# A two-layer decoder on one core: value products with the values as weights in the first attention, scores on four quarters of the array in the second cross attention, and new orders on every engine

## The chip, the core and the metric

The kernel runs on one core of a Trainium2 chip. The core has five engines that run their own instruction streams in order and meet at semaphores: TensorE (PE; its weight loads are shown apart as PEld), VectorE (DVE), ScalarE (ACT), GpSimd (POOL) and SyncE (SP), whose queue issues nearly all transfers here. The metric is device time in microseconds (us), the median of several executions. Lower is better.

## The reference

Input x is 16 batches of 64 tokens of 128 numbers. Two layers, each of three blocks, each with a layer norm ahead and a residual addition behind:

```
x = x + L0_attn(ln(x))          # causal self attention
x = x + L0_xattn(ln(x), ctx)    # one head of 128, no mask
x = x + L0_ffn(ln(x))           # 8 experts + a shared one, top 2 per token
x = x + L1_attn(ln(x))          # state space scan, gelu, layer norm
x = x + L1_xattn(ln(x), ctx)    # 8 heads of 64, key mask, projection
x = x + L1_ffn(ln(x))           # 8 experts; each takes its best tokens
```

Two of them matter here. In the first attention the 64 x 384 projections of a batch are reshaped to 16 heads, so that a head is 64 positions of 24 numbers (8 each for query, key, value):

```
qkv = (ln(x) @ W + b).reshape(b, 16, s, 24)        # q, k, v of 8 each
attn = softmax(q @ k.T * scale + causal)
out = (attn @ v).reshape(b, s, 128)
```

The second cross attention:

```
q, k, v = x @ W_q, ctx @ W_k, ctx @ W_v           # 8 heads of 64
sim = where(mask, q @ k.T * scale, -max)
out = (softmax(sim) @ v) @ W_o + b_o
```

## The kernel before

X holds all 1024 tokens on the chip as 8 tiles of 128 tokens (a tile is two batches), and half h is tiles 4h to 4h + 3. PSUM is used as eight banks of 128 x 512 floats, named bank[0] to bank[7]. Every engine's program is a list of calls of small functions, written out by hand; the order of that list is the order of the instructions, and a `wait_ge` in a function holds everything behind it on that engine. There is no scheduler.

**First attention.** It runs over eight pairs m of batches. The unit of softmax is u = 2m + u2, eight of the 16 heads of pair m: a 128 x 512 block whose partitions are two batches of 64 and whose columns are eight heads of 64. PE computes scores (L758) onto a causal bias (L749), one call for both units of a pair. DVE takes the row maximum (row_max, L1843) and subtracts it (subtract_max, L1850). ACT takes the exponentials (L1413). PE transposes them in four 128 x 128 blocks (transpose_probs, L776), always into bank 4, so that transpose_probs(u) waits until ACT has copied u - 1 out (copy_probs, L1419). Then weigh_values(u) (L792) multiplies: the probabilities of two batches by 64 positions are the weights (128 rows by 64 columns), and the moving side is Vb, the values of a head with a column of ones behind them (VW = 9 columns for each of two batches, block diagonal), 18 columns. Its output has query positions on partitions. The ones give the softmax's sum; DVE takes its reciprocal (inverse, L1829) and multiplies (normalise, L1835) into att.

Position and head then have to change places to give tokens. This goes through DRAM, once for each half: outputs_by_feature(h) transposes on PE (L804), ACT copies (L1427), SP stores to o_scratch (L418) in pieces of 128 bytes and loads back to OT (L421); outputs_by_token(h) transposes on PE (L822), and add_attention(h) on DVE adds to X (L1856). Between the two round trips SP issues the weights of the last FFN (1 MB of W1, L425, and eight pieces of W2, L427).

**Second cross attention.** It runs over the tiles t. scores1(t) starts a bank with one matmul that spreads the mask over 128 rows (L971: maskrow, on one partition, 512 columns) and adds 16 products of 64 x 64 (L976), two batches by eight heads. Head 2hp + h2 has its query and key on partition half h2 and its output on the same half h2, so of the four 64 x 64 quarters of the array only the two on the diagonal are used. DVE subtracts the row maximum (subtract_max1, L1954 and L1957) and, behind ACT's exponentials (L1488), adds up and inverts (probs1, L1964 and L1965); POOL multiplies (weigh_probs, L529); PE transposes into bank 2 (L986), ACT copies, PE multiplies by the values (weigh_values1, L999), ACT copies, PE projects (project_out, L1014) into bank 5 or 7, and DVE adds to X (add1, L1970). The DVE step that makes maskrow from the mask's bytes (mask_row, L1790) stands in DVE's list behind add_attention(1).

**Last FFN.** The choice of tokens is a search for a threshold for each expert: count (L1068) on PE and a chain of small DVE steps alternate 16 times. PE's list puts three or four up1 (L1029) or sixteen down1 (L1041) products between two counts. Behind the search DVE adds 56 weighted parts (L2042).

## Time and profile before

| what | value |
|---|---|
| three executions | 256.94, 257.46 (median), 261.43 us |
| the profiled execution: span | 255.3 us, 5508 instructions |
| median less the profiled span | 2.16 us |
| PE busy | 239.0 us (94%) |
| DVE busy | 175.9 us (69%) |
| ACT busy | 141.8 us (56%) |
| POOL busy | 77.9 us (31%) |

The profile is of one execution. Busy time is that of an engine's own instructions; a share over the span mixes stages with different limits, so the rows below are taken from stages. A group of rows in a timeline puts together instructions of one line that follow each other closely, with their count. Most fp32 matmuls of the program appear as two records (two passes), so a count in the trace is twice that of the program there; transposes appear once.

### The profile page before, as it was taken

What the parts mean: (1) busy time and instruction counts of PE and PEld (TensorE: products, weight loads), DVE (VectorE), ACT (ScalarE), POOL (GpSimd) and SP (SyncE); (2) the same over time, 40 slices, a digit from 0 to 9 for tenths busy, and PEclk for the clock granted to TensorE, in tenths of its full rate; (3) what the DMA queues carried; (4) which work ended last, traced back from release to release, by engine and by line L of the source; (5) the groups of instructions that cost most, each with busy time, mean ns of one, the idle gap of its engine ahead of it and who ended that gap; (6) DMA issues with size and microseconds to landing.
All of it is one profiled execution on the core that took longest, in us unless ns stands there. A gap on an engine that the chain in (4) does not pass through costs nothing.

```text
span 255.3 us, 5508 instructions
## 1 busy us (share of the span) xinstructions
PE 239.0 (94%) x1993; PEld 163.9 (64%) x1994; DVE 175.9 (69%) x602; ACT 141.8 (56%) x293; POOL 77.9 (31%) x137
## 2 busy tenths in 40 slices
PE   8988899998999999999999886999998999999995
PEld 8555577774535766756593534678887566577775
DVE  5465699874878836445217979957655688889975
ACT  0764776764264688467657445465565744544540
POOL 7856900001040474667465051533401000000000
DMA  5888960178100000000000000000000000000002
GB/s 136 173 196 245 302 152 0 31 220 205 44 1 0 1 3 0 0 1 3 0 1 3 1 0 0 3 3 3 3 5 0 3 0 0 1 3 0 0 3 82
DMA packets 24040, 11.64 MB, mean 46 GB/s; under 512 B 13017, under 2 KB 23006, under 8 KB 24014
## 3 DMA queue, kind: packets, MB, share of 16 engines
q1 hardware_dynamic: 22973, 10.94, 16.5%
q0 software_dynamic: 80, 0.20, 0.7%
q8 instruction: 16, 0.26, 0.4%
q10 hardware_dynamic: 960, 0.16, 0.3%
q14 instruction: 11, 0.08, 0.1%
HBM read 8.68 MB, written 2.62 MB: 44 GB/s over the span
## 4 chain that ended last, share of the span: by engine, by line
PE 73%; DVE 15%; ACT 5%; issue 3%; POOL 2%; DMA 1%; DVEq 0%; POOLq 0%; ACTq 0%
PE bank L1029 10%; PE bank L1041 10%; PE bank L897 6%; PE bank L884 6%; PE bank L916 6%; PE bank L776 3%; DVE stats L1720 3%; PE bank L1014 3%; PE bank L758 2%; PE bank L976 2%; PE bank L648 2%; PE bank L792 2%; PE bank L693 2%; PE bank L986 2%; PE bank L999 2%
## 5 line engine op out<-in xcount | busy, mean ns | idle before, releaser
L516 POOL TENSOR_TENSOR X<-X,att 128x128 f32<-128x128 f32 x72 | 30.4, 457 | 29.2 <-ACT att L1469 29.1
L441 POOL TENSOR_TENSOR rs<-rs,halves 128x4 f32<-128x4 f32 x14 | 14.9, 1063 | 61.8 <-DVE rs L1735 61.1
L1029 PE MATMUL bank<-XT,Wb 128*128 128x512 f32 x64 | 29.9, 599 | 0.0
L1041 PE MATMUL bank<-Wb,att 128*128 128x128 f32 x224 | 27.2, 278 | 0.0
L1041 PEld LDWEIGHTS bank<-Wb,att 128*128 128x128 f32 x224 | 26.1, 192 | 1.4 <-issue 1.4
L1905 DVE SCALAR_TENSOR_TENSOR att<-bank,cols,att 128x512 f32<-128x512 f32 x18 | 13.5, 749 | 16.8 <-ACT att L1458 7.8
L1469 ACT ACTIVATE att<-bank,comb 128x128 f32<-128x128 f32 x72 | 20.2, 383 | 6.9 <-PE bank L916 6.8
L1509 ACT ACTIVATE att<-bank 128x512 f32<-128x512 f32 x32 | 18.7, 599 | 9.7 <-PE bank L1029 9.7
L916 PEld LDWEIGHTS bank<-W2a,att 128*128 128x128 f32 x144 | 18.0, 192 | 5.0 <-issue 3.6
L916 PE MATMUL bank<-W2a,att 128*128 128x128 f32 x144 | 18.7, 276 | 0.0
L884 PE MATMUL bank<-XT,W1a 128*128 128x512 f32 x36 | 18.2, 595 | 0.0
L897 PE MATMUL bank<-XT,W3a 128*128 128x512 f32 x36 | 18.1, 598 | 0.0
L1517 ACT ACTIVATE big<-bank 128x512 f32<-128x512 f32 x14 | 8.3, 596 | 17.1 <-PE bank L1041 17.1
L1458 ACT ACTIVATE att<-bank,cols 128x512 f32<-128x512 f32 x18 | 12.6, 699 | 9.5 <-DVE att L1905 7.1
L1029 PEld LDWEIGHTS bank<-XT,Wb 128*128 128x128 f32 x64 | 11.2, 192 | 9.4 <-issue 8.8
L2042 DVE SCALAR_TENSOR_TENSOR X<-big,rt,X 128x128 f32<-128x128 f32 x56 | 15.4, 347 | 2.6 <-ACT big L1517 2.4
L1742 DVE TENSOR_SCALAR XN<-X,mv,rs 128x128 f32<-128x128 f32 x48 | 14.1, 356 | 4.1 <-POOL rs L441 3.8
L1720 DVE BATCH_NORM_STATS2 stats<-X 128x6 f32<-128x128 f32 x48 | 10.4, 280 | 7.1 <-POOL X L516 5.3
L1419 ACT ACTIVATE PTs<-bank 128x512 f32<-128x512 f32 x16 | 9.5, 595 | 8.0 <-PE bank L776 5.8
L529 POOL TENSOR_TENSOR Es<-Es,sm 128x512 f32<-128x512 f32 x8 | 8.2, 1044 | 14.2 <-DVE sm L1965 14.2
L1843 DVE TENSOR_REDUCE mx<-bank 128x8 f32<-128x512 f32 x16 | 10.5, 678 | 2.4 <-PE bank L758 2.4
L776 PE MATMUL bank<-ident,Es 128*128 128x128 f32 x64 | 10.2, 283 | 1.9 <-ACT PTs L1419 1.6
(229 smaller groups left out, 484.1 us busy)
## 6 DMA issues: line engine op xcount, KB each, us to landing
Wb<-in_L_ffn_W SPq DMA_DIRECT2D x1, 1024.0 KB, 5.5
Wb<-in_L_ffn_W SPq DMA_DIRECT2D x8, 128.0 KB, 5.2
X<-in_x SPq DMA_DIRECT2D x2, 256.0 KB, 3.1
k_scratch<-QKVT SPq DMA_DIRECT2D x1, 512.0 KB, 3.9
q_scratch<-QKVT SPq DMA_DIRECT2D x1, 512.0 KB, 4.7
Wb<-k_scratch SPq DMA_DIRECT2D x1, 512.0 KB, 4.6
v_scratch<-QKVT SPq DMA_DIRECT2D x1, 512.0 KB, 6.1
V<-q_scratch SPq DMA_DIRECT2D x1, 512.0 KB, 6.2
```

Of the source, the lines that this page charges most:

```text
L441: nc.gpsimd.tensor_tensor(rs[:, 0, cut], rs[:, 1, cut], halves[:, :], ALU.pow).then_inc(l_root[h], 1)
L516: nc.gpsimd.tensor_tensor(X[:, h * HT + t, :], X[:, h * HT + t, :], part0[:, i % 2, t, :], ALU.add).then_inc(f_acc, 1)
L776: last = nc.tensor.transpose(bank[4][:, p4 * P:(p4 + 1) * P], Es[:, u % 3, p4 * P:(p4 + 1) * P], ident[:, :])
L884: mm(bank[i % 2][:, :], W1a[:, e, :], XT[:, half(h)], start=True, stop=True).then_inc(f_h1, 1)
L897: mm(bank[2 + i % 2][:, :], W3a[:, e, :], XT[:, half(h)], start=True, stop=True).then_inc(f_h3, 1)
L916: last = mm(bank[4 + i % 2][:, t * P:(t + 1) * P], hid0[:, i % 2, t * P:(t + 1) * P], W2a[:, e, :], start=not shared, stop=True, skip_grou ...
L1029: mm(bank[i % 4][:, :], W1b[:, e, f * P:(f + 1) * P], XT[:, half(h)], start=True, stop=True).then_inc(m_up, 1)
L1041: last = mm(bank[4 + h][:, t * P:(t + 1) * P], hid[:, e % 2, f, tile], W2b[:, e, f, :], start=(f == 0), stop=(f == F1 - 1))
L1469: AF(part0[:, i % 2, t, :], bank[4 + i % 2][:, t * P:(t + 1) * P], ACT.Copy, scale=comb[:, tt, e:e + 1]).then_inc(f_part, 1)
L1509: AF(hid[:, e % 2, f, half(h)], bank[i % 4][:, :], ACT.Gelu).then_inc(m_gelu, 1)
L1720: last = V.bn_stats(stats[:, t, :], src[:, t, :])
L2042: last = V.scalar_tensor_tensor(X[:, t, :], ys[:, e, t, :], rt[:, 9, t, e:e + 1], X[:, t, :], ALU.mult, ALU.add)
```

## The change

**Value products turned.** weigh_values now runs once for each pair m. The values of a head, padded to VW = 16 columns for each of two batches, are the weights (128 rows by 32 columns), and the probabilities of 64 queries move. Four heads at a time go into four groups of 32 output partitions of bank 6. The output has value numbers on partitions, so the softmax's sum is one of the rows. inverse, normalise and outputs_by_feature are gone. ACT copies the 128 x 256 result (values_out) into OV, whose rows are stored as they stand: 512 KB for each half instead of 256. Four loads bring each half back, two with the outputs and two with the sums. sums_by_token(h) transposes the sums on PE (four small blocks), sums_inverse(h) takes the reciprocals on DVE, and add_attention(h) first multiplies into XN and then adds. transpose_probs alternates between banks 4 and 5.

**Four quarters in scores1.** Banks 0 to 3 become two twins of two banks. scores1(t) writes tile t into twin t % 2: h2 selects the bank, and a second index j the half of the output partitions, so that the four quarters are used. The bias becomes four matmuls of 64 rows by 256 columns, and maskrow is on 128 partitions. DVE reads both banks in one instruction. Transposes move to bank 4, products by the values to banks 5 and 6, and projections have bank 7 alone.

**Orders.** Every list is written anew around this. On DVE mask_row moves from behind add_attention(1) into the first FFN, and probs1(0) ahead of subtract_max1(1). On POOL the clearing of att (now all 4096 columns) comes later, and the additions of the output bias come behind weigh_probs(2). On ACT the widening of queries and the laying out of values for the second cross attention come earlier. In the last FFN one up1 fewer precedes the first count, and three gaps between counts hold three up1 products instead of four.

The core of the diff:

```diff
-    VW = HD + 1
+    VW = 16
...
+        twin = [ctx.enter_context(nc.psum_tensor(f"bank{2 * i}", [P, 2, 512], fp32)) for i in range(2)]
+        bank = [twin[i // 2][:, i % 2, :] for i in range(4)]
+        bank += [ctx.enter_context(nc.psum_tensor(f"bank{i}", [P, 512], fp32)) for i in range(4, 8)]
...
+        OV = [big[:, first:first + N].rearrange("p (c y t m) -> p m y c t", c=CH, m=HT, t=GT) for first in (12 * N, 15 * N)]
...
+        SU = big[0:CH, 14 * N:15 * N]
...
-        o_d = nc.dram_tensor("o_scratch", [2, P, HALF], fp32).ap()
+        o_d = nc.dram_tensor("o_scratch", [2, P, N], fp32).ap()
...
         def out_bank(t):
-            return 5 if t < HT else (5, 7)[t % 2]
+            return 7
...
-                sp.wait_ge(o_act[h], 1)
-                sp.dma_start(o_d[h, :, :].rearrange("(c e) (b u x) -> e b u c x", e=HD, b=HB, u=2)
-                             .rearrange("e b u c x -> (e b u) c x"), OT2).then_inc(st_o[h], 16)
+                sp.wait_ge(a_out, HT * (h + 1))
+                sp.dma_start(o_d[h, :, :], OVrows[h]).then_inc(st_o[h], 16)
...
-                sp.dma_start(OT[:, half(h)], o_d[h, :, :]).then_inc(ld_o[h], 16)
+                blocks = o_d[h, :, :].rearrange("(j n v) (c x) -> n v c j x", j=NP4, n=2, c=CH)
+                for n in range(2):
+                    sp.dma_start(OT[:, half(h)].rearrange("p (n j x) -> p n j x", n=2, j=NP4)[:, n, :, :],
+                                 blocks[n, 0:HD, :, :, :].rearrange("e c j x -> (e c) j x")).then_inc(ld_o[h], 16)
+                for n in range(2):
+                    sp.dma_start(SU[:, half(h)].rearrange("c (n j x) -> c n j x", n=2, j=NP4)[:, n, :, :],
+                                 blocks[n, HD, :, :, :]).then_inc(ld_s[h], 16)
...
-                if u >= 1:
...
+                if u >= 2:
+                    pe.wait_ge(a_trc, u - 1)
...
-                    last = nc.tensor.transpose(bank[4][:, p4 * P:(p4 + 1) * P],
+                    last = nc.tensor.transpose(bank[4 + u % 2][:, p4 * P:(p4 + 1) * P],
...
-            def weigh_values(u):
-                pe.wait_ge(a_trc, u + 1)
...
+            def weigh_values(m):
+                pe.wait_ge(a_trc, 2 * m + 2)
...
-                if u >= 2:
-                    pe.wait_ge(a_norm, u - 1)
-                for p4 in range(NP4):
-                    for g2 in range(2):
-                        head = (u % 2) * 2 * NP4 + 2 * p4 + g2
-                        last = mm(bank[5 + u % 2][g2 * S:(g2 + 1) * S, p4 * 2 * VW:(p4 + 1) * 2 * VW],
-                                  PTs[:, u % 2, p4 * P + g2 * S:p4 * P + (g2 + 1) * S],
-                                  Vb[:, u // 2, head, :, :].rearrange("p n v -> p (n v)"), start=True, stop=True)
+                if m >= 1:
+                    pe.wait_ge(a_out, m)
+                for i in range(NP4):
+                    for j in range(NP4):
+                        head = NP4 * j + i
+                        u2, first = head // HD, (head % HD) * S
+                        last = mm(bank[6][j * 2 * VW:(j + 1) * 2 * VW, i * S:(i + 1) * S],
+                                  Vb[:, m, head, :, :].rearrange("p n v -> p (n v)"),
+                                  PTs[:, u2, first:first + S], start=True, stop=True)
...
+            def sums_by_token(h):
+                pe.wait_ge(ld_s[h], 32)
...
+                for t in range(HT):
+                    last = nc.tensor.transpose(bank[7 - 2 * h][:, t * CH:(t + 1) * CH],
+                                               SU[:, half(h)].rearrange("c (x m) -> c m x", m=HT)[:, t, :], ident[0:CH, 0:CH])
+                last.then_inc(o_sums[h], 1)
...
-                dst = bank[t % 2]
-                bias = per_col(maskrow[0:1, t * P:(t + 1) * P], NHP)
-                mm(dst[:, :], onesb[0:1, :], bias, start=True, stop=False, skip_group_check=True)
-                for hp in range(NHP):
+                for h2 in range(2):
+                    rows = slice(h2 * S, (h2 + 1) * S)
+                    bias = per_col(maskrow[rows, t * P:(t + 1) * P], NHP // 2)
+                    for j in range(2):
+                        mm(bank[2 * (t % 2) + h2][j * S:(j + 1) * S, 0:2 * P], onesb[rows, 0:S], bias,
+                           start=True, stop=False, skip_group_check=True)
+                for i in range(NHP // 2):
                     for b2 in range(2):
-                        for h2 in range(2):
-                            tok = slice(t * P + b2 * S, t * P + (b2 + 1) * S)
-                            last = mm(dst[h2 * S:(h2 + 1) * S, (2 * hp + b2) * S:(2 * hp + b2 + 1) * S],
-                                      Q1T[h2 * DH1:(h2 + 1) * DH1, hp, tok], K1T[h2 * DH1:(h2 + 1) * DH1, hp, tok],
-                                      start=False, stop=(hp == NHP - 1), skip_group_check=True)
+                        tok = slice(t * P + b2 * S, t * P + (b2 + 1) * S)
+                        for j in range(2):
+                            for h2 in range(2):
+                                rows, hp = slice(h2 * DH1, (h2 + 1) * DH1), 2 * i + j
+                                last = mm(bank[2 * (t % 2) + h2][j * S:(j + 1) * S, (2 * i + b2) * S:(2 * i + b2 + 1) * S],
+                                          Q1T[rows, hp, tok], K1T[rows, hp, tok],
+                                          start=False, stop=(i == NHP // 2 - 1), skip_group_check=True)
...
-                    last = nc.tensor.transpose(bank[2][:, hp * P:(hp + 1) * P],
+                    last = nc.tensor.transpose(bank[4][:, hp * P:(hp + 1) * P],
...
+                if t == 0:
+                    pe.wait_ge(c_qc[1], 4)
+                else:
...
-                if 1 <= t <= HT:
+                if t == 0:
+                    pe.wait_ge(c_qc[1], 4)
+                else:
                     pe.wait_ge(c_added, t)
-                if t == HT + 1:
-                    pe.wait_ge(c_qc[1], 4)
-                if t > HT + 1:
-                    pe.wait_ge(c_added, t - 1)
...
-                    act.wait_ge(a_pv, n - 1)
-                AF(PTs[:, n % 2, :], bank[4][:, :], ACT.Copy).then_inc(a_trc, 1)
...
+            def values_out(m):
+                act.wait_ge(a_pv, m + 1)
+                AF(OV[m // HT][:, m % HT, :, :, :], bank[6][:, 0:2 * P].rearrange("p (y c t) -> p y c t", c=CH, t=GT), ACT.Copy
+                   ).then_inc(a_out, 1)
...
-            def inverse(u):
-
-                dve.wait_ge(a_pv, u + 1)
-                V.reciprocal(rO[:, u, :].rearrange("p (a n) -> p a n", n=2), weights(u)[:, :, :, HD]).then_inc(a_inv, 1)
-
...
+            def sums_inverse(h):
+                dve.wait_ge(o_sums[h], 1)
+                V.reciprocal(rO[:, h, :, :], bank[7 - 2 * h][:, 0:HT * CH].rearrange("p (t c) -> p t c", c=CH)
+                             ).then_inc(o_inv[h], 1)
...
+                dve.wait_ge(o_inv[h], 1)
+                then(V.tensor_tensor(XN[:, tiles(h), :].rearrange("p t (c e) -> p t c e", e=HD),
+                                     bank[7 - h][:, :].rearrange("p (t e c) -> p t c e", e=HD, c=CH),
+                                     rO[:, h, :, :].unsqueeze(3).broadcast_to([P, HT, CH, HD]), ALU.mult))
...
-                s = bank[t % 2][:, :].rearrange("p (a s) -> p a s", s=S)
-                then(V.tensor_reduce(sm[:, t, 0, :], s, AX.X, ALU.max))
+                s = twin[t % 2][:, :, 0:2 * P].rearrange("p h (a s) -> p h a s", s=S)
+                then(V.tensor_reduce(sm[:, t, 0, :].rearrange("p (h a) -> p h a", h=2), s, AX.X, ALU.max))
...
```

On PE in the loop of the first attention, before (line 776 transposes probabilities, 749 and 758 make scores, 792 multiplies by the values):

```order
L776 MATMUL bank<-ident,Es 128x128 x4
L749 MATMUL bank<-causal,perm 128x512 x2
L758 MATMUL bank<-big,Wb 128x4x64 x4
L776 MATMUL bank<-ident,Es 128x128 x4
L792 MATMUL bank<-att,PTs 64x18 x16
L776 MATMUL bank<-ident,Es 128x128 x4
```

and in the changed kernel (790 transposes, 761 and 770 scores, 806 value products):

```order
L790 MATMUL bank<-ident,Es 128x128 x8
L761 MATMUL bank<-causal,perm 128x512 x2
L770 MATMUL bank<-big,Wb 128x4x64 x4
L806 MATMUL bank<-PTs,att 32x64 x16
L790 MATMUL bank<-ident,Es 128x128 x8
```

Both units of a pair are now transposed in one row, and the scores of a later pair stand between them and their value products.

On PE at the end of the first attention, before (822 is outputs_by_token(0), 767 keep_busy, 804 outputs_by_feature(1)):

```order
L822 MATMUL bank<-ident,OT 128x128 x4
L776 MATMUL bank<-ident,Es 128x128 x4
L792 MATMUL bank<-att,PTs 64x18 x8
L776 MATMUL bank<-ident,Es 128x128 x4
L792 MATMUL bank<-att,PTs 64x18 x16
L767 MATMUL bank<-causal,perm 128x512 x2
L804 MATMUL bank<-ident,att 128x128 x4
L648 MATMUL bank<-ident,XN 128x128 x4
```

and now (818 is sums_by_token(0), 836 outputs_by_token(0), 681 and 684 are keys and values of the second cross attention):

```order
L806 MATMUL bank<-PTs,att 32x64 x16
L818 MATMUL bank<-ident,big 128x16 x4
L836 MATMUL bank<-ident,OT 128x128 x4
L790 MATMUL bank<-ident,Es 128x128 x8
L806 MATMUL bank<-PTs,att 32x64 x16
L681 MATMUL bank<-maskf,Wk 128x512
L684 MATMUL bank<-Wv,CTXT 128x512
L681 MATMUL bank<-maskf,Wk 128x512
L660 MATMUL bank<-ident,XN 128x128 x4
```

The transposes by feature are gone, the small transposes of the sums stand ahead of outputs_by_token(0), and keys and values follow the last products at once.

On DVE at the start of the second cross attention, before (1954 and 1957 are subtract_max1, 1742 a layer norm of the other half, 1964 and 1965 probs1):

```order
L1954 TENSOR_REDUCE sm<-bank 128x8
L1957 TENSOR_TENSOR Es<-bank,sm 128x512
L1742 TENSOR_SCALAR XN<-X,mv,rs 128x128 x4
L1954 TENSOR_REDUCE sm<-bank 128x8
L1957 TENSOR_TENSOR Es<-bank,sm 128x512
L1964 TENSOR_REDUCE sm<-Es 128x8
L1965 RECIPROCAL sm<-sm 128x8
```

and now (2029, 2032, 1827, 2040 and 2041 are the same steps):

```order
L2029 TENSOR_REDUCE sm<-bank 128x8
L2032 TENSOR_TENSOR Es<-bank,sm 128x512
L1827 TENSOR_SCALAR XN<-X,mv,rs 128x128 x4
L2040 TENSOR_REDUCE sm<-Es 128x8
L2041 RECIPROCAL sm<-sm 128x8
L2029 TENSOR_REDUCE sm<-bank 128x8
L2032 TENSOR_TENSOR Es<-bank,sm 128x512
```

The sums of tile 0 come ahead of the maximum of tile 1.

## Rows read from the trace of the kernel before

**Rows 1.** The page: the chain that ended last, shares of the span by engine.
```profile
PE 73%; DVE 15%; ACT 5%; issue 3%; POOL 2%; DMA 1%; DVEq 0%; POOLq 0%; ACTq 0%
```
**Rows 2.** Windows: length, PE, PEld, DVE, ACT, POOL busy (instructions), clock, DMA share, GB/s.
```profile
26.50:59.30 32.80, 30.23 (x414) 23.31 (x416) 27.85 (x75) 21.43 (x39) 6.14 (x5) 1.00 0.56 146
...
134.00:155.00 21.00, 17.60 (x64) 8.04 (x63) 17.74 (x72) 12.27 (x25) 7.01 (x9) 1.00 0.01 1
155.00:189.40 34.40, 32.38 (x633) 26.17 (x633) 24.81 (x67) 19.19 (x40) 11.52 (x11) 1.00 0.01 3
189.40:255.30 65.90, 62.37 (x365) 43.72 (x363) 51.23 (x221) 30.42 (x51) 1.01 (x1) 1.00 0.03 9
```
**Rows 3.** Lines of PE, 26.5 to 59.3: busy us, mean ns, idle before.
```profile
L776 PE MATMUL bank<-ident,Es 128*128 128x128 f32 x64 | 10.2, 283 | 1.9 <-ACT PTs L1419 1.6 <-ACT Es L1413 0.4
L792 PE MATMUL bank<-att,PTs 128*64 128x18 f32 x256 | 9.8, 213 | 0.6 <-DVE att L1835 0.4
L758 PE MATMUL bank<-big,Wb 64*128 64x256 f32 x64 | 8.3, 379 | 0.7 <-ACT Wb L1391 0.7
L749 PE MATMUL bank<-causal,perm 64*128 64x512 bf16 x14 | 2.7, 386 | 0.0
...
L804 PE MATMUL bank<-ident,att 128*128 128x128 f32 x4 | 0.6, 272 | 0.0
```
**Rows 4.** Lines of DVE and of ACT in the same stretch.
```profile
L1850 DVE TENSOR_TENSOR Es<-bank,mx 128x512 f32<-128x512 f32 x16 | 10.6, 679 | 0.6 <-PE bank L776 0.4
L1843 DVE TENSOR_REDUCE mx<-bank 128x8 f32<-128x512 f32 x16 | 10.5, 678 | 2.4 <-PE bank L758 2.4
L1835 DVE TENSOR_TENSOR att<-bank,rO 128x64 f32<-128x64 f32 x15 | 3.4, 259 | 0.2
L1829 DVE RECIPROCAL rO<-bank 128x8 f32<-128x8 f32 x16 | 3.0, 194 | 2.5 <-PE bank L792 2.5
...
L1413 ACT ACTIVATE Es<-Es 128x512 f32<-128x512 f32 x16 | 9.6, 627 | 2.4 <-DVE Es L1850 2.2
L1419 ACT ACTIVATE PTs<-bank 128x512 f32<-128x512 f32 x16 | 9.5, 595 | 8.0 <-PE bank L776 5.8 <-PE bank L792 2.1
...
L1427 ACT ACTIVATE big<-bank 128x256 f32<-128x256 f32 x2 | 0.7, 384 | 0.0
```
**Rows 5.** Timeline (start us, us, instructions of a group): small products on PE.
```profile
63.76 0.73 PE L837 MATMUL bank<-K0T,QKVT 128*64 128x64 f32 x16
...
126.69 0.43 PE L928 MATMUL bank<-XT,BT 128*32 128x128 f32 x8
...
165.06 0.69 PE L999 MATMUL bank<-PTs,big 64*64 64x64 f32 x32
```
**Rows 6.** Timeline: weights, second round trip, addition to X, maskrow.
```profile
53.06 5.13 SPq L427 DMA_DIRECT2D Wb<-in_L_ffn_W  x8
...
61.23 0.37 SPq L418 DMA_DIRECT2D o_scratch<-big  x1
...
64.19 0.34 SPq L421 DMA_DIRECT2D OT<-o_scratch  x1
...
67.91 0.68 DVE L1856 TENSOR_TENSOR X<-bank,X 128x512 f32<-128x512 f32 x1
...
73.17 0.67 DVE L1790 TENSOR_SCALAR maskrow<-masku 1x1024 bf16<-1x1024 uint8 x1
```
**Rows 7.** Lines of PE, 155.0 to 189.4: scores1 and its bias.
```profile
L976 PE MATMUL bank<-big,att 64*64 64x64 f32 x256 | 9.2, 221 | 0.0
...
L971 PE MATMUL bank<-maskrow,onesb 1*128 1x512 bf16 x8 | 3.1, 383 | 2.6 <-DVE Es L1957 1.7 <-ACT att L1484 1.0
```
**Rows 8.** Timeline of PE in the last FFN: first and last count, products between.
```profile
199.43 0.25 PE L1068 MATMUL bank<-hit,onesb 128*128 128x192 bf16 x1
199.51 1.91 PE L1029 MATMUL bank<-XT,Wb 128*128 128x512 f32 x4
...
229.00 0.26 PE L1068 MATMUL bank<-hit,onesb 128*128 128x192 bf16 x1
```

## What I expect of the change, and why

> **What bounds the kernel now.** I read first the page's chain that ended last: its shares by engine show that for 73% of the span the chain runs over PE, for 15% over DVE and hardly over a DMA [rows 1]. The reader is to see there that PE's time is the first place to look for a gain, but that an average over eight stages says nothing of one stage. So the second view is the windows by stage, where busy time of each engine stands against the length of the stretch [rows 2]. In the first attention's loop (26.5 to 59.3) PE is busy 30.23 of 32.80 us and DVE 27.85; in the second cross attention (155.0 to 189.4) PE 32.38 of 34.40 and DVE 24.81; in the last FFN (189.4 to the end) PE 62.37 of 65.90. The state-space stage between 134 and 155 is held by neither (17.60 and 17.74 of 21.00), so by waits. The granted clock is 1.00, the 2.4 GHz level, in all of them.
>
> The third view is the lines of one engine in one stretch. In the attention loop PE's work is four groups: transposes of probabilities 10.2, value products 9.8, scores 8.3 and their causal bias 2.7 [rows 3]. DVE and ACT have their own lines in the same stretch [rows 4]. There are eight pairs of batches, so by pair: PE 30.23 / 8 = 3.78 us; DVE 2 x (0.679 + 0.678 + 0.194 + 0.259) = 3.62 us; ACT 2 x (0.627 + 0.595) = 2.44 us. The length is 32.80 / 8 = 4.10 us a pair. PE and DVE are both close to it; a gain on one alone would be lost on the other.
>
> **The value products.** Before, a pair costs 9.8 / 8 = 1.22 us for 32 matmul records with 18 moving columns. After, it is 32 records again (16 in the program, two passes each), now with 32-column weights in four column groups and 64 moving columns. No row of before has this shape. Nearest is L999, 32 records with 64 moving columns on four quarters of the array: 0.69 us [rows 5]. L928 has the same weights, 128 rows by 32 columns, in four column groups with 128 moving columns: eight records in 0.43 us, 54 ns each, where four records of 128 columns at full width (L804) take 0.6, 150 ns each; so groups of this kind do run side by side [rows 3, 5]. The far bound is L837, 64 moving columns with 64-column weights: 16 records in 0.73, so 1.46 for 32. I take 0.69: 8 x 0.69 = 5.5, a gain on PE of 9.8 - 5.5 = 4.3 us; at the far bound a loss of 8 x 1.46 - 9.8 = 1.9.
>
> DVE loses 16 reciprocals and 16 products (3.0 and 3.4 us, one record of the latter missing). ACT gains one copy of 128 x 256 a pair, 0.38 by L1427, and loses those copies behind the old transposes [rows 4]. PE loses eight transposes (L804, two groups of 0.6) and gains eight with 16 rows, which I count at half: another -0.6. By pair this leaves PE (30.23 - 4.3 - 0.6) / 8 = 3.17, ACT 2.44 + 0.38 = 2.82, DVE 2 x (0.679 + 0.678) = 2.71. PE still leads, so PE's 4.9 us is the upper bound of the gain, but three engines are now within 0.5 us of each other.
>
> Here a page speaks against the change. The Trainium skill, "TensorEngine Tiling (Array Packing)", Performance Considerations, PSUM Bottleneck, says that packing the array speeds up TensorE but not the emptying of PSUM, which may then bound. By the rows just summed it would not bound, since DVE's part falls too; by the rule read strictly the attention gains nothing, and that is rival B.
>
> **The round trip of the second half.** The outputs go through DRAM to get tokens onto partitions, and the first FFN needs that of half 1. So I follow it as a chain [rows 6]. Before: store issued at 61.23, load at 64.19 (2.96 for the store), the addition to X at 67.91 (3.72 for load, transposes and wait). After: the store no longer waits for the L804 transposes (0.6) and two ACT copies (0.76), and the last products are 4.3 earlier: 61.23 - 0.6 - 0.76 - 4.3 = 55.6; plus values_out 0.38, 55.95. It carries 512 KB instead of 256, but in whole rows; between nothing and another 2.96 more I take 1.0. Four loads are issued where one was: 3 x 0.34 = 1.0 more. So 55.95 + 2.96 + 1.0 + 1.0 + 3.72 = 64.6 against 67.91: **-3.3 us**. The additional multiply ahead of the addition (one pass like L1856, 0.68) is paid by mask_row, which leaves DVE's chain there (0.67). All this is behind the eight weight loads of L427 on the SP queue (5.13 us of issuing); they must have been issued by 55.95, and before they were by 53.06 + 5.13 = 58.2. Their start is released by the last scores and the first round trip, which both move earlier by about half of the gain, so this wait is between 0 and 2 us; the 1.0 for the store holds its middle. What covers the chain on PE is the keys and values of the second cross attention; PE reaches outputs_by_token(1) before the loads have landed and loses there 4.9 - 3.3 = 1.6 us. So the stage is worth between 0 (rival B) and -4.9, and I take -3.3.
>
> **The second cross attention.** Scores (L976) cost 9.2 us on PE and their bias (L971) 3.1, together 12.3 or 1.54 a tile [rows 7]. After, the scores have L999's shape and its four quarters (0.69), and the bias is four matmuls of 256 columns, two by two side by side; by half of L971's 0.383 that is 0.2. So 8 x (0.69 + 0.2) = 7.1, PE -5.2 us. How much comes through? DVE needs 24.81 of 34.40, so it has room. But of the 2.6 us that PE waited ahead of L971, 1.7 were for DVE's subtraction, and the output products now have a single bank, so project_out(t) waits for the addition of the tile before. Against that each tile gets a pair of banks, so that PE can run a tile ahead of DVE. I take half: **-2.6**, bounds 0 and -5.2. The new orders ahead of it (the widening of queries earlier on ACT, probs1(0) ahead of subtract_max1(1) on DVE, weigh_probs ahead of add_bias on POOL) I cost at nothing: in 134 to 155 they lie in the idle 3.26 us of DVE and 3.40 of PE; uncovered, one 128 x 512 pass is 0.68.
>
> **The last FFN.** The search's counts run from 199.43 to 229.00, fifteen steps of 1.97 us, filled with products [rows 8]. One product fewer (0.48, by four in 1.91) lies ahead of the first count, and three of the gaps are filled with three products instead of four. PE is the bound (62.37 of 65.90), and the same products are done; only the wait ahead of the last count and at the end can shrink. **-0.5**, bounds 0 and one step, -1.97.
>
> **Sum.** -3.3 - 2.6 - 0.5 = -6.4 us. The profiled span 255.3 becomes 248.9; the median 257.46 lies 2.16 above the span, and I keep that: 251.1 us.
>
> **Rivals.** A is the forecast. **B: the attention loop stays as long**, because ACT and DVE set it: ACT now has a copy of the pair between two copies of probabilities, and transposes wait for it. For it: the three sums by pair are within 0.5 us. Against: none reaches 4.10. Then 257.46 - 2.6 - 0.5 = 254.4. **C: the second cross attention stays as long**, by one output bank and DVE's chain per tile; for it speaks that 1.7 of PE's 2.6 us of waits there are DVE's, against it that DVE has 9.6 us free: 257.46 - 3.3 - 0.5 = 253.7. **The column groups run one after the other**: L837's price, PE +1.9 - 0.6 = +1.3 in the attention, 257.46 + 1.3 - 3.1 = 255.7; L928 speaks against it. I count it with B. **E: both PE gains come through whole** (and nothing in the last FFN): 257.46 - 4.9 - 5.2 = 247.4. **D, slower: TensorE falls to the 1.2 GHz level** when PE stalls at the round trip of half 1 (about 1.6 us at outputs_by_token(1)) or loses its long products. Every us of PE work there then costs a us more, and it decides from 251.1 + 11.5 = 262.6 on: 11.5 us of work, less than half of the attention's 25. Against it: PE waited 2.6 us ahead of eight L971 groups, and the granted clock is 1.00 in each stretch. The Trainium skill, "TensorE: Matmul & The Clock Gate", Part 4 (PE-mode transpose), says that transposes don't engage the full clock as other matmuls do, and the share of transposes grows here; the row with 10.2 us of them at clock 1.00 does not show it.
>
> **How the numbers follow.** A 0.55 (248.5 to 254, of which 0.42 below 252.3), E 0.10, B with serial groups 0.18, C 0.10, D 0.07. About 2% (5.1 us) is what a measurement of this kernel can tell from no change, so faster is below 252.3: 0.42 + 0.10 = 0.52. B, C and the upper part of A are within 2%: 0.18 + 0.10 + 0.13 = 0.41. Slower is D, 0.07. The range leaves out D, half of E and the case in which B and C come together (257.0, part of their chances): 247.5 to 256.5.
>
> **What would show it.** Value products: 32 records in about 0.69 us (0.6 to 0.9 right, above 1.2 the serial rival). Attention: PE still busy over 85% between first scores and last products; if ACT or DVE is over 95%, B. Round trip: addition to X of half 1 near 64.6. Scores of the second cross attention: 0.7 a tile and bias 0.2, with DVE over 80% busy in a stretch of about 32 us; if the stretch is 34 and DVE still 72%, C by latency. Granted clock 1.00 throughout; 0.5 to 0.9 in any stretch is D. I am wrong if a stretch that I cost at nothing (state-space stage, first FFN) is over 1 us longer or shorter.

## The result, and the profile after

Median of 20 executions each: 257.42 us before, 254.44 after; ratio 0.9872, 95% interval 0.9845 to 0.9899. So the change is worth 3.0 us, 1.3%; 251.1 was forecast. The profiled execution's span fell from 255.3 to 252.1.

One thing has to be known to read the numbers below: the granted clock differs between executions of the same kernel. Of the changed kernel's 20, ten have a mean clock of 1.00 and spans of 251.5 to 252.1; the others have 0.973 to 0.993 and up to 257.3. The kernel before does the same: of 58 of its executions, taken beside the experiments, 23 have 0.999 or 1.00 and spans of 255.2 to 255.8 (median 255.2), the others 0.98 to 0.993 and up to 259.5. So spans at 1.00 are compared where tenths matter, and by the medians at 1.00 (255.2 and 251.6) the change is worth 3.6.

The windows by stage of the changed kernel (columns as in [rows 2]):

```profile
26.50:54.90 28.40, 25.29 (x419) 19.44 (x417) 24.29 (x42) 22.62 (x44) 5.07 (x4) 1.00 0.63 176
...
131.60:154.40 22.80, 19.09 (x81) 9.89 (x81) 19.21 (x76) 12.39 (x26) 5.79 (x8) 1.00 0.00 1
154.40:186.80 32.40, 28.08 (x657) 22.52 (x658) 23.51 (x65) 19.36 (x40) 12.74 (x12) 1.00 0.01 3
```

The attention loop lost 4.4 us of its 32.80, and the second cross attention 2.0 of 34.40, though PE lost 4.3 there. These windows begin and end with PE's work; between the first and the last step of DVE in the second cross attention the gain is only 0.7, as will be seen. PE's lines that answer to [rows 3, 7]:

```profile
L806 PE MATMUL bank<-PTs,att 128*32 128x64 f32 x256 | 5.2, 222 | 1.6 <-ACT PTs L1468 1.5
...
L995 PE MATMUL bank<-big,att 64*64 64x64 f32 x256 | 5.1, 218 | 0.0
L987 PE MATMUL bank<-maskrow,onesb 64*64 64x256 bf16 x32 | 2.4, 280 | 2.3 <-DVE Es L2032 1.4 <-issue 0.8
```

Value products fell from 9.8 to 5.2 us and scores from 9.2 to 5.1. Where that went is seen by following the same steps through both timelines:

| step (start, us) | before | after | shift |
|---|---|---|---|
| last value products, PE | 58.61 | 54.29 | -4.3 |
| second store issued, SP | 61.23 | 55.64 | -5.6 |
| transposes of the outputs of half 1, PE | 67.10 | 63.16 | -3.9 |
| addition to X of half 1, DVE | 67.91 | 65.92 | -2.0 |
| first down product of the first FFN, PE | 83.96 | 82.28 | -1.7 |
| X of half 1 complete (its statistics, DVE) | 135.66 | 133.91 | -1.8 |
| maximum of tile 0, second cross attention, DVE | 157.50 | 155.73 | -1.8 |
| last addition of that block, DVE | 189.53 | 187.04 | -2.5 |
| last addition of the kernel, DVE | 252.7 | 249.5 | -3.2 |

So in these two executions the first attention is worth 1.8 in the end, the second cross attention 0.7, and the last FFN 0.7. That is the 3.2 between the spans of 255.3 and 252.1; this execution of the changed kernel is the longest of the ten at 1.00, and the table behind the experiments shows why. The two rows of DVE that bound the second cross attention, before and then after:

```profile
157.50 0.68 DVE L1954 TENSOR_REDUCE sm<-bank 128x8 f32<-128x512 f32 x1
...
189.53 0.29 DVE L1970 TENSOR_TENSOR X<-bank,X 128x128 f32<-128x128 f32 x1 [0.60 <-PE bank L1014]
```
```profile
155.73 0.68 DVE L2029 TENSOR_REDUCE sm<-bank 128x8 f32<-128x512 f32 x1
...
187.04 0.29 DVE L2046 TENSOR_TENSOR X<-bank,X 128x128 f32<-128x128 f32 x1 [2.06 <-PE bank L1032]
```

The loss in the first attention lies between the second and the fourth row of the table. The timeline of that round trip:

```profile
55.64 0.34 SPq L420 DMA_DIRECT2D o_scratch<-big  x1
60.32 0.92 SPq L424 DMA_DIRECT2D OT<-o_scratch  x2
61.28 0.97 SPq L427 DMA_DIRECT2D big<-o_scratch  x2
63.16 0.75 PE L836 MATMUL bank<-ident,OT 128*128 128x128 f32 x4 [0.77 <-DMA OT<-o_scratch]
63.84 0.65 PE L818 MATMUL bank<-ident,big 16*128 16x16 f32 x4
64.53 0.56 DVE L1910 RECIPROCAL rO<-bank 128x64 f32<-128x64 f32 x1 [0.39 <-PE bank L818]
65.19 0.69 DVE L1929 TENSOR_TENSOR XN<-bank,rO 128x512 f32<-128x512 f32 x1
65.92 0.69 DVE L1932 TENSOR_TENSOR X<-XN,X 128x512 f32<-128x512 f32 x1
```

The store takes 4.68 us until the loads may be issued (2.96 in [rows 6]), and behind the transposes of the outputs stand the small transposes, the reciprocal and the multiply, one after the other: 2.76 us to the addition, where it was 0.81.

### The profile page after: what moved, and what is told of

It is laid out like the page before. It is cut to its first block, busy times and chain, and to the rows that moved or that the text cites. A ratio compares the mean times of both kernels' runs of the same rounds, so it can differ in the third digit from the quotient of the medians.

```text
span 252.1 us, 5538 instructions
## 1 busy us (share of the span) xinstructions
PE 231.0 (92%) x2018; PEld 157.2 (62%) x2018; DVE 172.7 (68%) x574; ACT 142.3 (56%) x297; POOL 78.9 (31%) x137
## 4 chain that ended last, share of the span: by engine, by line
PE 36%; DVE 12%; POOL 2%; ACT 2%; issue 1%; DVEq 0%
PE bank L1047 11%; PE bank L1059 10%; PE bank L930 2%; PE bank L1032 2%; PE bank L911 2%; DVE stats L1805 2%; PE bank L969 2%; PE bank L898 1%; PE bank L1005 1%; PE bank L1019 1%; DVE sm L2029 1%; DVE XN L2005 1%; DVE XN L1827 1%; PE bank L1086 1%; POOL Es L537 1%
## 5 line engine op out<-in xcount | busy, mean ns | idle before, releaser
L448 POOL TENSOR_TENSOR rs<-rs,halves 128x4 f32<-128x4 f32 x14 | 14.3, 1022 | 79.7 <-DVE rs L1820 63.8
L1552 ACT ACTIVATE att<-bank 128x512 f32<-128x512 f32 x32 | 18.0, 601 | 8.4 <-PE bank L1047 8.1
L1379 ACT ACTIVATE XT<-bank 128x512 f32<-128x512 f32 x12 | 7.2, 601 | 8.2 <-PE bank L660 8.2
L1922 DVE TENSOR_TENSOR Es<-bank,mx 128x512 f32<-128x512 f32 x16 | 10.4, 683 | 0.1
```

Of the source, the lines that this page charges most:

```text
L448: nc.gpsimd.tensor_tensor(rs[:, 0, cut], rs[:, 1, cut], halves[:, :], ALU.pow).then_inc(l_root[h], 1)
L1552: AF(hid[:, e % 2, f, half(h)], bank[i % 4][:, :], ACT.Gelu).then_inc(m_gelu, 1)
```

## The experiments

Each is the changed kernel with one edit, except the eighth.

**Groups one after the other.** In weigh_values:

```diff
-                for i in range(NP4):
-                    for j in range(NP4):
+                for j in range(NP4):
+                    for i in range(NP4):
```

> The changed kernel with the two loops of weigh_values exchanged: four products in a row go to the same 32-column group, and then to the next, instead of going round the four groups. Theory PACKING: the 0.65 us of a pair's 32 records come from products in different column groups lying over each other, so in one group at a time they need more, towards the 1.46 of twice L837's row: 1.0 to 1.5 us a pair, 3 to 6 us over eight pairs on PE, of which most shows in the last value product (54.3 in the changed kernel) and at most 2 to 3 in the span, as the stretches behind it have idle PE time. Theory ISSUE: the 0.65 us are 32 times the time to issue one product, and the order of the groups is all the same: 0.6 to 0.7 again, span within 0.4 of 252.1.

Span 257.1 at clock 1.00, median 259.01. The same pair in the changed kernel and in this one, from the timelines:

```profile
47.57 0.65 PE L806 MATMUL bank<-PTs,att 128*32 128x64 f32 x32
```
```profile
47.44 1.39 PE L806 MATMUL bank<-PTs,att 128*32 128x64 f32 x32
```

PACKING holds: 0.74 us a pair more, 5.9 in all, of which 5.5 reached the span (257.1 against 251.6, the median of the changed kernel's ten), more than the 2 to 3 expected. It also tells that the turned products alone, without the round over the groups, would have been no gain on PE (1.39 against 1.22 before). The Trainium skill, "TensorEngine Tiling (Array Packing)", Key Properties, says that different tiles can load and multiply in parallel; the two rows agree, and show that the order of the products decides whether they do.

**Quarters one after the other.** In scores1 the loops over j and h2 go outside:

```diff
-                for i in range(NHP // 2):
-                    for b2 in range(2):
-                        for j in range(2):
-                            for h2 in range(2):
+                for j in range(2):
+                    for h2 in range(2):
+                        for i in range(NHP // 2):
+                            for b2 in range(2):
```

> The changed kernel with the loops of scores1 exchanged: the four products of one quarter of the array follow each other, then those of the next quarter. The bias and the layout stay. Theory PACKING: 0.65 us of a tile become 1.15 (the two quarters of the kernel before) to 2; PE's work in the stretch grows by 4 to 10 us and the stretch (32.4) by half of it or more, 2 to 5. Theory ISSUE: 0.65 stays and the span is within 0.4 of 252.1.

A tile's scores take 1.49 us instead of 0.66, and the span at 1.00 is 255.5 to 256.1. PE's line in the list of groups:

```profile
L995 PE MATMUL bank<-big,att 64*64 64x64 f32 x256 | 11.6, 223 | 0.0
```

The window of the second cross attention:

```profile
153.80:190.10 36.30, 33.74 (x656) 28.66 (x657) 23.60 (x65) 19.05 (x40) 12.74 (x12) 1.00 0.01 2
```

The scores cost PE 6.5 us more, PE's busy time in the window grew by 5.7 and the window by 3.9 (between the two steps of DVE by 3.7, 34.98 against 31.31). PACKING holds, and PE is busy for nearly the whole stretch again.

**Less work on PE there.** The four bias products of each tile are left out.

```diff
-                for h2 in range(2):
-                    rows = slice(h2 * S, (h2 + 1) * S)
-                    bias = per_col(maskrow[rows, t * P:(t + 1) * P], NHP // 2)
-                    for j in range(2):
-                        mm(bank[2 * (t % 2) + h2][j * S:(j + 1) * S, 0:2 * P], onesb[rows, 0:S], bias,
-                           start=True, stop=False, skip_group_check=True)
...
-                                          start=False, stop=(i == NHP // 2 - 1), skip_group_check=True)
+                                          start=True, stop=True)
```

> The changed kernel without the four bias products (L987) of each tile in the second cross attention, so without the key mask (the result of that block is therefore another); everything else is the same. PE loses 2.4 us of busy time there. Theory PE: PE still sets the stretch, as the slower scores of the serial experiment (PE +6.5 us, span +3.5) suggest, and the span at clock 1.00 falls by 1.0 to 2.0, to 249.7 to 250.8. Theory CHAIN: behind the change the per-tile chain through DVE, ACT, POOL and PE sets it, and the span falls by less than 0.5.

All ten executions had a clock below 1.00 (at most 0.993, span from 252.5), so the spans do not decide. The stretch does, in which this execution's clock was 1.00. First maximum and last addition in DVE's timeline:

```profile
158.25 0.68 DVE L2023 TENSOR_REDUCE sm<-bank 128x8 f32<-128x512 f32 x1
...
189.54 0.29 DVE L2040 TENSOR_TENSOR X<-bank,X 128x128 f32<-128x128 f32 x1 [2.07 <-PE bank L1026]
```

The window over them:

```profile
158.20:189.60 31.40, 26.77 (x561) 20.94 (x562) 22.36 (x58) 18.54 (x39) 12.75 (x12) 1.00 0.01 3
```

31.29 us, against 155.73 to 187.04 = 31.31 with the bias. The stretch hardly varies, 31.31 or 31.32 in the six other profiled executions that leave this block as it is, but for filler, and keep a clock of 1.00 in it. So PE's 2.4 us are worth nothing: CHAIN. The chain that ended last in the two profiles says the same. Of this stretch, PE holds 27.3 us of it before and 16.8 in the changed kernel, DVE 3.2 and 7.2, ACT and POOL together 0.6 and 4.9.

**Less work on DVE there.**

```diff
-                then(V.tensor_reduce(sm[:, t, 0, :].rearrange("p (h a) -> p h a", h=2), s, AX.X, ALU.max))
+                then(V.tensor_reduce(sm[:, t, 0, :].rearrange("p (h a) -> p h a", h=2), s[:, :, :, 56:64], AX.X, ALU.max))
```

> The changed kernel with the row maximum of the second cross attention taken over the last 8 of the 64 keys instead of all (a softmax is the same whatever is subtracted, as long as nothing overflows), so that L2029 costs about 0.2 us instead of 0.66 for each of eight tiles: 3.6 us less on DVE, everything else the same. Theory DVE: of the 4.35 us that PE gained in the second cross attention only 0.7 came through (by DVE's rows: subtract_max1(0) 1.77 earlier than before, the last addition 2.49 earlier), because DVE's chain per tile bounds it; then the last addition comes 2 to 3.6 us earlier than 187.04. Theory BANK: the single bank of project_out and the chain of PE and ACT bound it: earlier by less than 1.

The maximum took 0.195 us instead of 0.66. The one execution at clock 1.00 had 251.3, against 251.5 to 252.1: 0.2 to 0.8 for 3.7 us of DVE, from a single execution. The profiled one lost its clock inside the stretch (0.50 at 160 to 162) and does not count. As far as one execution tells, DVE's busy time by itself is not the bound either.

**Orders of the state-space stage.** From the end of the first FFN to the first scores, the lists of the kernel before on PE, and on DVE and ACT from the states on (the first piece below is PE's, the second ACT's). ACT's last silu of the first FFN kept its new place behind a weigh0, so this is not a clean return: DVE waited 3.31 us for it.

```diff
-            down0(1, 6)
             up0_first(1, 8)
-            down0(1, 7)
-            up0_third(1, 8)
             inject(0)
-            down0(1, 8)
+            up0_third(1, 8)
+            down0(1, 6)
             widen(0, 0)
+            down0(1, 7)
             widen(0, 1)
+            down0(1, 8)
             widen(0, 2)
...
-            copy_xt(3, 1, 6)
-            state(1, 0)
-            state(1, 1)
             keys_values1(8)
             keys_values1(9)
-            state(1, 2)
-            state(1, 3)
-            gelu_states(1)
             keys_values1(10)
             keys_values1(11)
+            copy_xt(3, 1, 6)
+            state(1, 0)
+            state(1, 1)
+            state(1, 2)
...
```

> The changed kernel (span 252.1, median 254.4) with the orders of the kernel before on PE, ACT and DVE between the last products of the first FFN and the first scores of the second cross attention: inject(0) and its widenings stand between the last down0 products again, and states_moments(0) ahead of ln_apply(3, 1). In the changed kernel the first FFN ends 1.8 us earlier than before (131.4 against 133.2) but the first bias of the scores starts only 0.3 earlier (154.43 against 154.74), so the stretch grew by 1.5. Theory ORDER: the growth is the new order, because inject(0) starts at 129.1 instead of 126.7 and DVE reaches the gelu's statistics of half 0 only at 137.55 (137.06 before). Then the first bias comes at 152.9 to 153.3, and the span falls by 1.1 to 1.5, to about 250.8. Theory DVE: DVE is full there whatever the order (19.2 busy of 22.8), and the first bias stays at 154.0 to 154.6, the span within 0.4 of 252.1.

The first bias came at 155.68, later than in either kernel. By itself that does not decide, since the way from the addition to X of half 1 to the statistics below had already become 3.0 us longer (65.56 to 136.60, against 65.92 to 133.91). What decides is seen in DVE's rows, from the statistics of X of half 1 to the end of the last addition of states. Changed kernel, and then this one:

```profile
133.91 0.86 DVE L1805 BATCH_NORM_STATS2 stats<-X 128x6 f32<-128x128 f32 x4
...
153.61 0.69 DVE L2023 TENSOR_TENSOR X<-QKVT,X 128x512 f32<-128x512 f32 x1
```
```profile
136.60 0.87 DVE L1805 BATCH_NORM_STATS2 stats<-X 128x6 f32<-128x128 f32 x4 [1.29 <-POOL X L524]
...
156.29 0.69 DVE L2023 TENSOR_TENSOR X<-QKVT,X 128x512 f32<-128x512 f32 x1
```

153.61 + 0.69 - 133.91 = 20.39 and 156.29 + 0.69 - 136.60 = 20.38; before it was 155.38 + 0.69 - 135.66 = 20.41. DVE's chain has one length in all three orders, so ORDER falls. The stretch from the last down product to the first scores grew (22.80 against 21.00 in the windows) because products moved across its border, PE's busy time in it from 17.60 to 19.09; by DVE's chain nothing was lost in it.

**Weights late.** The nine loads of the last FFN's weights are issued behind the second round trip, not behind the first.

```diff
-                if h == 0:
+                if h == 1:
                     sp.wait_ge(a_scores, NU)
```

> The changed kernel with the nine loads of the last FFN's weights issued behind the second round trip instead of between the two. In the changed kernel the first store of outputs takes 3.37 us until the loads may issue (43.35 to 46.72) and the second 4.68 (55.64 to 60.32), while the weights are still landing. Theory CONTENTION: the second store takes 3.3 to 3.5 us here, outputs_by_token(1) starts at about 62.3 instead of 63.16 (it then waits for PE's filler), the addition to X of half 1 moves from 65.92 to about 65.3, and the span falls by 0.3 to 0.8. Theory SIZE: the second store is as long for another reason (512 KB, behind the values copy), 4.5 or more, and nothing moves.

SP's timeline:

```profile
58.05 0.34 SPq L420 DMA_DIRECT2D o_scratch<-big  x1
60.69 0.93 SPq L424 DMA_DIRECT2D OT<-o_scratch  x2
```

The store then takes 2.64 us instead of 4.68: CONTENTION, not size, though the store is twice as large as before the change. Other profiled executions agree. Where the weights are in flight this store takes 3.60 to 4.68 (eight kernels), and where they are not, 2.64 or 2.65 (four). The profiled execution lost its clock twice (0.50 to 0.61 at 26 to 30 and 54 to 58) and so tells nothing of the addition; the one execution at 1.00 had 251.7. No gain by this alone.

**Sums first.** With the weights late, the sums are loaded and transposed ahead of the outputs.

```diff
-            outputs_by_token(1)
             sums_by_token(1)
+            outputs_by_token(1)
             keep_busy(4, 2)
```

> The changed kernel with the weights of the last FFN loaded behind the second round trip, the sums loaded ahead of the outputs in both round trips, and sums_by_token(1) ahead of outputs_by_token(1) on PE. In the changed kernel the addition to X of half 1 starts 2.76 us after its outputs' transposes (63.16 to 65.92; before 67.10 to 67.91, 0.81), because the small transposes, the reciprocal and a multiply follow one another. Theory TAIL: this is the give-back of the round trip; with the sums first, the small transposes and the reciprocal lie ahead of the outputs, the addition starts 1.5 to 1.7 us after the outputs' transposes, at 64.6 to 65.2, and the span falls by 0.5 to 1.2 at clock 1.00 (251.5 to 252.1 in the changed kernel's executions). Theory COVERED: PE's work bounds the stretch up to the first FFN (15.83 of 16.60 busy), and the span moves by less than 0.3.

DVE's rows:

```profile
63.77 0.43 DVE L1946 TENSOR_TENSOR QKVT<-QKVT,sm 128x256 f32<-128x256 f32 x1
64.11 0.55 DVE L1910 RECIPROCAL rO<-bank 128x64 f32<-128x64 f32 x1
...
65.49 0.69 DVE L1932 TENSOR_TENSOR X<-XN,X 128x512 f32<-128x512 f32 x1
```

The addition came at 65.49, not 64.6 to 65.2, and two executions at 1.00 had 251.7. The reciprocal started only at 64.11 although its input was there at 63.03 (transposes 62.38, 0.65): it stands behind cross0_prob(0), whose last step is L1946, in DVE's list. The span stayed as under COVERED, but by DVE's order, not by PE.

**No tail.** In half 1 the outputs are added undivided: add_attention keeps its multiply for h == 0 alone, and the reciprocal of half 1 is gone.

```diff
+                else:
+                    then(V.tensor_tensor(X[:, tiles(h), :].rearrange("p t (c e) -> p t c e", e=HD),
+                                         bank[7 - h][:, :].rearrange("p (t e c) -> p t c e", e=HD, c=CH),
+                                         X[:, tiles(h), :].rearrange("p t (c e) -> p t c e", e=HD), ALU.add))
...
-            sums_inverse(1)
```

> The changed kernel without the division by the softmax's sums in half 1 of the first attention: add_attention(1) adds the undivided outputs to X at once, without the reciprocal and the multiply and without waiting for the sums (half 0 is divided as before; the result of half 1 is therefore another). This takes the tail of the second round trip away: the addition should start at 64.2 instead of 65.92. Theory TAIL: the first FFN and all behind it follow the addition, and the span at clock 1.00 falls by 1.2 to 1.7, to 250.0 to 250.6. Theory COVERED: PE's work up to the first FFN takes most of it, and the span falls by less than 0.6.

DVE's row:

```profile
63.92 0.68 DVE L1935 TENSOR_TENSOR X<-bank,X 128x512 f32<-128x512 f32 x1
```

The addition started at 63.92, 2.0 earlier than in the changed kernel's profile. But 0.6 of that is not the tail's: the store took 3.60 us in this execution and 4.68 in that one. Against the execution with the scores one after the other, where the store took 3.62 and the addition came at 65.29, the tail is worth 1.4. Three executions at 1.00 had 250.4, 250.5 and 251.0: 1.1 less than 251.6, the median of the changed kernel's ten. TAIL, with most of it coming through.

**The last FFN's order alone**, in the kernel before (the counts as in the change, all else old).

> The kernel before with only the changed order of the last FFN (on PE and ACT from the first count on); everything ahead is the kernel before. By the traces this order's part is 0.7 us: the first count comes 0.84 earlier against its route, the search takes 2.0 longer (31.6 against 29.6), and the part behind it is 1.9 shorter. Theory SUM: span 254.4 to 254.8 against 255.2 to 255.4 at clock 1.00, so the parts add up. Theory NONE: 255.0 to 255.5, and the 0.7 belong to the shift of what lies ahead.

254.5 at clock 1.00 against 255.2: the 0.7 that the milestones gave. SUM.

**No filler.**

```diff
-            keep_busy(4, 2)
             cross0_scores(0)
-            keep_busy(4, 3)
             outputs_by_token(1)
             sums_by_token(1)
-            keep_busy(4, 2)
```

> The changed kernel without the seven filler products (keep_busy, L779) around the second round trip, 2.0 us of PE. Nothing is computed with them. Theory CLOCK: PE's waits then become 2 to 4 us long, the granted clock falls to 0.50 behind them for some us, and the span is longer by 1 to 3. Theory WORK: the filler costs time; without it the span falls by 0.5 to 1 and the clock stays at 1.00.

None of ten executions reached 1.00 (0.960 to 0.987); median 257.07. That is CLOCK's forecast. PE's timeline:

```profile
60.80 0.73 PE L851 MATMUL bank<-K0T,QKVT 128*64 128x64 f32 x16 [0.78 <-ACT QKVT L1474]
62.52 0.74 PE L836 MATMUL bank<-ident,OT 128*128 128x128 f32 x4 [0.99 <-DMA OT<-o_scratch]
...
64.99 1.97 PE L868 MATMUL bank<-V,QKVT 64*64 64x128 f32 x16 [0.47 <-ACT QKVT L1483]
66.89 2.07 PE L681 MATMUL bank<-maskf,Wk 96*128 96x512 f32 x2
```

Windows of two us over it:

```profile
64.00:66.00 2.00, 1.44 (x12) 1.21 (x14) 1.86 (x4) 0.38 (x1) 0.00 (x0) 0.71 0.00 0
66.00:68.00 2.00, 2.00 (x12) 1.15 (x9) 1.90 (x11) 0.00 (x0) 0.38 (x1) 0.50 0.03 8
```

Behind waits of 0.78, 0.99 and 0.47 the clock is 0.50, the 1.2 GHz level, and L868 takes 1.97 us instead of 1.09. The waits are shorter than the 2 to 4 us expected.

**Waits filled.** 23 filler products where PE waited, without a wait of their own (shown without the six ahead of scores1(0) and queries1(1, 0)):

```diff
             transpose_probs(13)
+            filler(0, 3)
             weigh_values(6)
             sums_by_token(0)
+            filler(0, 3)
             outputs_by_token(0)
             transpose_probs(14)
             transpose_probs(15)
+            filler(0, 3)
             weigh_values(7)
...
             keep_busy(4, 3)
+            filler(4, 3)
             outputs_by_token(1)
...
             scores1(1)
+            filler(4, 5)
             scores1(2)
```

> The changed kernel with filler products (as L779, results unused) put where PE waited in its profile: three each ahead of weigh_values(6), outputs_by_token(0) and weigh_values(7) (waits of 0.74), three more ahead of outputs_by_token(1) (0.77), three ahead of scores1(0) (0.84), five ahead of scores1(2) (1.43) and three ahead of queries1(1, 0) (0.69). In the experiment without filler the granted clock fell in every execution (0.987 at most), in the changed kernel in about half of them (1.00 in 9 or 10 of 20), each fall costing 0.8 to 2 us. Theory CLOCK: the falls follow on waits of PE, so filled waits make them rare: clock 1.00 in most executions, their span 251.5 to 252.3, and the median 253.3 to 253.8 instead of 254.4. Theory CHANCE: the falls have another cause, and about half of the executions keep them; then the median stays at 254.4 or more, as the filler may delay what follows.

Four of five executions at 1.00 (251.6 to 251.8), median 253.51, ratio 0.984 (0.9803 to 0.9878). That agrees with CLOCK, on few executions.

**Filler and an early reciprocal together.** The filler just shown (without the three products ahead of outputs_by_token(1)), the late weights, the sums loaded first, and on PE sums_by_token(1) right behind cross0_scores(0). On DVE:

```diff
             cross0_sub(0)
+            sums_inverse(1)
             cross0_prob(0)
-            sums_inverse(1)
             add_attention(1)
```

> The changed kernel with three edits that the experiments point to: the filler of the filled-waits experiment (without the three ahead of outputs_by_token(1)), the weights of the last FFN behind the second round trip with the sums loaded ahead of the outputs, and sums_by_token(1) on PE and sums_inverse(1) on DVE moved ahead, so that the reciprocal lies ahead of cross0_prob(0). Without the division the addition started at 63.92 and the span fell by 1.1. Here only the multiply is left in the tail: the multiply at about 64.2, the addition at 64.9 instead of 65.92. Theory TAIL: span at clock 1.00 251.0 to 251.4, and with the filler the median is 252.8 to 253.3. Theory COVERED: 251.5 to 252.1 and 253.3 to 253.8, as in the filled-waits experiment.

Six executions, all with a clock of 0.999 or 1.00, 252.56 to 252.77; median 252.64, ratio to the kernel before 0.9794 (0.9744 to 0.9844). Its median is below those of both kernels (257.42 and 254.44, other executions). Its DVE rows:

```profile
62.35 0.55 DVE L1920 RECIPROCAL rO<-bank 128x64 f32<-128x64 f32 x1
...
63.93 0.68 DVE L1939 TENSOR_TENSOR XN<-bank,rO 128x512 f32<-128x512 f32 x1
64.64 0.69 DVE L1942 TENSOR_TENSOR X<-XN,X 128x512 f32<-128x512 f32 x1
```

The addition is at 64.64, 1.28 earlier than in the changed kernel's profile and 0.7 earlier than in the profile with the waits filled (65.36), and the span is 0.7 shorter (250.9 against 251.6): TAIL.

**The addition and the span.** Five profiled executions at clock 1.00 whose work behind this addition is the same, but for filler and for the time at which the weights are loaded:

| execution | second store takes | addition of half 1 starts | span | span less addition |
|---|---|---|---|---|
| changed kernel | 4.68 | 65.92 | 252.1 | 186.2 |
| waits filled | 4.03 | 65.36 | 251.6 | 186.2 |
| sums first | 2.64 | 65.49 | 251.7 | 186.2 |
| no tail | 3.60 | 63.92 | 250.4 | 186.5 |
| filler and early reciprocal | 2.64 | 64.64 | 250.9 | 186.3 |

What is gained at this addition reaches the span, all but 0.3 us. And one execution's store can mislead: the changed kernel's profile has the longest of all. With 3.62 to 4.37 us for it, four other kernels with the same steps on DVE start the reciprocal at 63.86 to 64.17 instead of 64.53, in most of them right behind cross0_prob(0), and the addition at 65.24 to 65.56. That fits the spans of the changed kernel at 1.00: 251.5 to 251.8 in nine executions, 252.1 in the profiled one.

## Why the prediction was right in direction and half in size

**Value products: right.** 0.69 forecast, 0.65 measured; the last products came the forecast 4.3 earlier. That L928's groups overlap was the right row; the serial rival is what the loop exchange makes of it. (The small transposes of the sums cost as much as those that they replace, 0.65 for four and not half.)

**The attention loop: right.** The middle pairs follow each other every 2.8 to 3.0 us (start of value products 36.18, 38.97, 41.98, 44.78, 47.57), below the 3.17 forecast for PE, and PE is busy for 89% of the loop, DVE for 86%. Rival B is out: the loop did not stay as long. The rule of the Trainium skill that stood behind B ("TensorEngine Tiling (Array Packing)", Performance Considerations, PSUM Bottleneck) did not come true here: DVE's busy time in the loop fell too, from 27.85 to 24.29.

**The round trip: the step that failed first.** Its issue was right to 0.3 (55.95 forecast, 55.64), with some luck, as values_out took 0.61 and not 0.38. The store was given 3.96 and took 4.68 in the profile, 3.60 to 4.37 in seven others; so the size was about right, but the reason was not. The extra 1.0 was meant for the doubled bytes, and these cost nothing that the runs show (2.64 without the weights; the first store, with no weights in flight, 2.62 to 3.52 against 2.99 before). What the store did pay for is the weights in flight. The four load issues, given 1.0, cost the outputs nothing, as theirs are issued first. What failed is the tail: "The additional multiply ahead of the addition ... is paid by mask_row" was wrong. mask_row stood behind the addition [rows 6], at 73.17, and could not pay for anything ahead of it; and the small transposes and the reciprocal were left out of the chain altogether. In the profile that is 2.76 - 0.81 = 1.95 us; in the executions with a shorter store DVE's order holds the reciprocal, and taking reciprocal and multiply away is worth 1.4. So the addition came 2.0 earlier in the profile and 2.3 to 2.7 in four others, instead of 3.3, and nearly all of that is in the span.

**The second cross attention: the step that failed most.** PE fell by 4.3 us (5.2 forecast; the bias costs 0.30 a tile, not 0.2). "I take half" came to 0.7 instead of 2.6. Rival C was right on the place, and partly on the cause: not the one output bank (PE never waits for an addition there) and not DVE's load (3.7 us less of it gave 0.2 to 0.8), but the chain of a tile through DVE, ACT, DVE, POOL, PE, ACT, PE, ACT, PE, on which PE's part fell from 27.3 to 16.8 us. More work on PE lengthened the stretch at once, less did not shorten it. Which link of the chain would have to be shortened stays open: ACT's and POOL's part was not tested, nor less work on two engines at once, nor a fourth buffer for the probabilities.

**The last FFN: right in size, but not by its parts.** -0.5 forecast, -0.7 measured, alone and as part. By the counts on PE (199.43 and 229.00 before, 196.08 and 227.65 now) and the two additions around them, the first count comes 0.9 us earlier behind the block ahead, the search takes 2.0 longer (31.57 instead of 29.57), and what follows it is 1.9 shorter. The prediction had the end shrink but not the search grow.

**The stretches costed at nothing: right.** The state-space stage is 1.8 us longer by PE's windows (22.80 against 21.00), which was named as a sign of being wrong; by DVE's chain, which decides there, it is the same (20.39 and 20.41). From the addition of half 1 to the statistics at its start it is 67.75 us before and 67.99 now.

**The clock: it fell in half of the executions, for a few us each, but not by the change.** Rival D priced one fall of 11.5 us of work, and the traces with falls show short ones. The kernel before has them too, in 35 of 58 executions, so they are no price of the new orders. The gain is 3.6 at clock 1.00 and 3.0 in the medians; the changed kernel's median of 20 lies just between its ten at 1.00 and the other ten.

## What to carry to other kernels

When a stage gets shorter, follow the same step through both timelines until the shift stops shrinking: a chain of small steps on the way (here transposes, a reciprocal and a multiply behind a load) can take more than half of it. A step can only be "paid" by one that stood ahead of the same event. One profile is one execution: how long a transfer took is read from several. Products on parts of the array overlapped here only where neighbours in the order went to different parts (0.65 against 1.39 us a pair), and on a stage in which engines hand over tile by tile, less work on one of them may be worth nothing though more of it costs at once.

## What the runs showed of the hardware

TensorE's granted clock fell behind waits of less than a microsecond, several near each other. In the profiled execution of the kernel without bias, PE's timeline:

```profile
50.29 0.65 PE L806 MATMUL bank<-PTs,att 128*32 128x64 f32 x32 [0.74 <-ACT PTs L1462]
...
52.27 0.72 PE L836 MATMUL bank<-ident,OT 128*128 128x128 f32 x4 [0.74 <-DVE rO L1904]
...
55.05 1.08 PE L806 MATMUL bank<-PTs,att 128*32 128x64 f32 x32 [0.69 <-ACT PTs L1462]
56.06 2.08 PE L681 MATMUL bank<-maskf,Wk 96*128 96x512 f32 x2
```

The window over its end:

```profile
54.00:56.00 2.00, 1.31 (x34) 0.84 (x32) 1.86 (x10) 0.74 (x2) 0.00 (x0) 0.50 1.16 300
```

The changed kernel has the same three waits and kept 1.00 in its profiled execution, so they alone do not decide it. Between the waits PE did almost only transposes (L818, L836 and L790 here; L836, L818 and L858 in the kernel without filler), and no run tells the two apart; the row of transposes at clock 1.00 on which the prediction relied, with other products between them, doesn't either. The clock differed between executions of one program, and what decides in which of them it falls stays open. It was 0.999 or 1.00 in 23 of 58 executions of the kernel before and in 10 of 20 of the changed kernel, in none of 10 without the filler and in none of 10 without the bias. The last has the filler and the same waits there, so a count of none in ten does not by itself show what the filler is worth; that the clock fell right behind the waits without it speaks for it. With the waits filled it was 0.999 or 1.00 in 10 of 11 (the last two filled kernels together), against 16 of 44 in the eight other experiments that keep the changed kernel's filler.
